# A Mamba-2 mixer and a LoRA dense layer on one core: one unit's transposes by VectorE in 32x32 blocks and through DRAM

## What is computed

```python
proj = einsum('bsd,ed->bse', layernorm(x), in_proj_w)       # gate | hs,B,C | dt
hBC  = silu(causal depthwise conv, 4 taps, of proj's middle part)
hs   = hBC[..., :8192].reshape(b, s, 128 heads, 64)         # B, C: 8 groups x 128
xch  = hs * softplus(dt)                                     # per token and head
Y_diag = (C B^T * L) @ xch          # in chunks of 128 tokens, L = decay, lower triangle
states = B^T @ (decay * xch)        # per chunk, then carried from chunk to chunk
Y_off  = C @ carried states * exp(A_cum)
Y = Y_diag + Y_off + hs * D
out = groupnorm(Y * silu(gate)) * norm_w @ out_proj_w.T
x = x + out; x = x + layernorm(x) @ (W + LoRA) + b
```

## Time and profile before

| what | value |
|---|---|
| median of 3 runs (lowest, highest) | 1605.16 us (1605.1, 1605.87) |
| span of the profiled execution | 1605.0 us |
| PE busy | 1583.5 us, 99% |
| DVE busy | 1264.2 us, 79% |
| ACT busy | 1163.1 us, 72% |
| POOL busy | 700.7 us, 44% |
| chain that ended last | PE 97%, DVE 1%, ACT 1% |
| mean granted TensorE clock | 0.998 of 2.4 GHz |
| DMA | 162.37 MB, mean 101 GB/s, q1 30.8% of the 16 engines |

### The profile page before, as it was taken

The page is one execution under the profiler, slowest core; times in us unless marked ns, Lnnn a source line. Parts: engine busy times, 40 slices in busy tenths (PEclk is TensorE's granted clock), DMA queues, the critical chain, the costliest instruction groups (busy, mean ns, idle before and its releaser), DMA issues.

```text
span 1605.0 us, 26714 instructions
## 1 busy us (share of the span) xinstructions
PE 1583.5 (99%) x9576; PEld 1346.1 (84%) x9576; DVE 1264.2 (79%) x1984; ACT 1163.1 (72%) x2027; POOL 700.7 (44%) x535
## 2 busy tenths in 40 slices
PE   7899999999999999999999999999999999999998
PEld 5688888888888888888888888888888888888887
DVE  6687777877778777887778877787877878788787
ACT  5887667776777677777687766777677767777753
POOL 2155444453444454354453544445344445435550
PEclk9999999999999999999999999999999999999999
DMA  4542322332323233332232232233232323223211
GB/s 151 192 145 86 122 89 83 112 112 73 112 97 114 73 109 95 98 106 92 99 108 97 86 122 89 83 112 112 73 112 99 113 73 109 99 92 112 93 44 53
DMA packets 86916, 162.37 MB, mean 101 GB/s; under 512 B 23040, under 2 KB 39424, under 8 KB 86528
## 3 DMA queue, kind: packets, MB, share of 16 engines
q1 hardware_dynamic: 86784, 160.66, 30.8%
HBM read 154.84 MB, written 5.77 MB: 100 GB/s over the span
## 4 chain that ended last, share of the span: by engine, by line
PE 97%; DVE 1%; ACT 1%; issue 0%; DMA 0%; SPq 0%; DVEq 0%; ACTq 0%
PE g_bank L778 10%; PE g_bank L780 9%; PE g_bank L779 9%; PE d_bank L797 7%; PE x_bank L778 7%; PE x_bank L780 7%; PE x_bank L779 7%; PE head_bank L786 5%; PE head_bank L804 5%; PE x_bank L836 4%; PE x_bank L837 4%; PE x_bank L835 4%; PE d_bank L837 4%; PE d_bank L835 4%; PE d_bank L836 4%; PE head_bank L812 3%
## 5 line engine op out<-in xcount | busy, mean ns | idle before, releaser
L1448 POOL TENSOR_TENSOR w_low<-raw,w_high 128x512 fp32r<-128x512 f32 x139 | 179.8, 1294 | 553.5 <-ACT w_high L1011 553.5
L1199 DVE SCALAR_TENSOR_TENSOR hs<-x_bank,cols,hs 128x1022 f32<-128x1022 f32 x189 | 241.6, 1278 | 129.7 <-ACT hs L1033 127.5
L1021 ACT ACTIVATE scores<-scores,tables 128x128 f32<-128x128 f32 x1024 | 312.4, 391 | 0.0
L1462 POOL TENSOR_TENSOR y<-y,gate 128x512 f32<-128x512 f32 x128 | 185.4, 1467 | 198.8 <-DVE y L1268 198.8
L1033 ACT ACTIVATE hs<-x_bank,cols 128x1024 f32<-128x1024 f32 x63 | 75.9, 1204 | 269.9 <-PE x_bank L780 269.9
L778 PE MATMUL g_bank<-x_high,w_high 128*128 128x512 f32 x624 | 250.8, 402 | 0.0
L779 PE MATMUL g_bank<-x_low,w_high 128*128 128x512 f32 x624 | 243.2, 390 | 0.0
L780 PE MATMUL g_bank<-x_high,w_low 128*128 128x512 f32 x624 | 243.1, 390 | 0.0
L778 PE MATMUL x_bank<-x_high,w_high 128*128 128x512 f32 x504 | 196.3, 390 | 0.1
L780 PE MATMUL x_bank<-x_high,w_low 128*128 128x512 f32 x504 | 196.1, 389 | 0.0
L779 PE MATMUL x_bank<-x_low,w_high 128*128 128x512 f32 x504 | 196.1, 389 | 0.0
(11 more groups left out here) (211 smaller groups left out, 3433.3 us busy)
## 6 DMA issues: line engine op xcount, KB each, us to landing
scores<-sums_dram SPq DMA_DIRECT2D x128, 512.0 KB, 4.8
raw<-w_in SPq DMA_DIRECT2D x144, 256.0 KB, 2.9
grown_rows<-grown_dram SPq DMA_DIRECT2D x256, 96.0 KB, 2.8
out_raw<-w_out SPq DMA_DIRECT2D x64, 256.0 KB, 3.4
mixed<-x SPq DMA_DIRECT2D x8, 256.0 KB, 5.1
out<-mixed SPq DMA_DIRECT2D x8, 256.0 KB, 2.0
table_dram<-table SPq DMA_DIRECT2D x2, 768.0 KB, 5.3
tables<-table_dram SPq DMA_DIRECT2D x30, 48.0 KB, 2.7
```

The source lines that it names most:

```text
L1021: op = s.activation(at, at, ACT.Relu, bias=col[:, r, c:c + 1], scale=-1.0)
L1199: v.scalar_tensor_tensor(out=hs[:, q % 2, :, i:], in0=x_bank[:, :, 0:SEQ - i], scalar=cols[:, q, TAPS - 1 - i:TAPS - i], in1=hs[:, q % 2, ...
L1448: pool.tensor_tensor(w_low[:, slot], raw[:, slot], w_high[:, slot].bitcast(F32), ALU.subtract)\
L1462: pool.tensor_tensor(y[:, b], y[:, b], gate[:, q % 2, b], ALU.mult).then_inc(y_ready, 1)
```

## The change

TensorE's `turn_hs` goes, except in the first unit (`turn_first`, `first_heads`). From the second unit on, VectorE transposes `hs` in 32x32 blocks in one instruction (`turn_blocks`), with the output ordered so that the four 32-token pieces m of every chunk lie together. It writes into the half of `hs` that the previous unit has left, after that unit's `skip`. SP stores this to DRAM (`store_blocks`, 128 rows of 4 KB). Four loads (`load_quads`, each 128 runs of 1 KB into 32 partitions) bring it back as `quads`, tokens on the partitions. `to_heads` now reads `quads` in SBUF, one product for each of the two heads over both batches. So `xdt` is ready for both batches at once.

The order moves with it. On VectorE the three taps are together, ahead of `carried_state`; `turn_blocks` follows `skip`; `to_heads` comes behind both scores, and `squares_of` behind `y_low_part`. On SP the store stands before the grown loads and the quad loads behind them; the first weight load of the unit after is moved ahead of the store. On ScalarE the silu of `hs` comes before the second `differences`, both `decays` come last, and tap 0 waits for the store two units back. TensorE waits for `carry_scaled` in `states`. The bias buffers share memory with `out_high` and `out_low` (not shown, with the changed argument lists).

```diff
@@ -34,6 +34,9 @@
 DMA_SCRATCH = 8192
+QUAD = 32
+QUADS = P // QUAD
+PER_HEAD = HEAD_DIM // QUAD
@@ -81,6 +84,13 @@
+def splits_after(g, last, j, by):
+    if j + by < UNITS:
+        return splits_of(g, last, j + by)
+    return [] if last else splits_of(g + 1, False, j + by - UNITS)
@@ -95,6 +105,7 @@
     dense_dram = scratch("dense_dram", [P, KT * HID])
+    blocks_dram = scratch("blocks_dram", [P, BATCH * SEQ])
@@ -618,13 +629,16 @@
         ident_r = sb("ident_r", [P, P], F32R)
-        bias_high, bias_low = sb("bias_high", [P, HID], F32R), sb("bias_low", [P, HID], F32R)
+        quads = sb("quads", [P, QUADS, BATCH, CHUNKS, QUAD])
+        bias_high, bias_low = out_high[:, 0], out_low[:, 0]
...
         chunk_in = [[sem(f"chunk_in{b}_{h}") for h in range(2)] for b in range(BATCH)]
+        blocks_turned, blocks_stored = sem("blocks_turned"), sem("blocks_stored")
+        moved = [sem(f"moved{m}") for m in range(QUADS)]
@@ -658,6 +672,10 @@
+        def blocks_of(k):
+            return hs[:, (k - 1) % 2].rearrange("p b n -> p (b n)")
@@ -688,6 +706,20 @@
+            def store_blocks(k):
+                sp.wait_ge(blocks_turned, k)
+                for m in range(QUADS):
+                    reached(sp, moved[m], 16 * (k - 1))
+                sp.dma_start(blocks_dram, blocks_of(k)).then_inc(blocks_stored, 16)
+            def load_quads(k):
+                sp.wait_ge(blocks_stored, 16 * k)
+                sp.wait_ge(xdt_ready, PAIR * k)
+                by_part = blocks_dram.rearrange("(a j) (m n) -> m j a n", a=QUADS, m=QUADS)
+                for m in range(QUADS):
+                    sp.dma_start(quads[m * QUAD:(m + 1) * QUAD].rearrange("p a b c i -> p a (b c i)"), by_part[m])\
+                      .then_inc(moved[m], 16)
@@ -714,14 +746,9 @@
                     ahead, second = unit(g, last, j + 1), unit(g, last, j + 2)
-                    if j + 1 < UNITS:
-                        splits = splits_of(g, last, j + 1)
-                    else:
-                        splits = [] if last else splits_of(g + 1, False, 0)
+                    splits = splits_after(g, last, j, 1)
...
                         first_dense(sp)
-                    for at in splits[:1]:
-                        load_weight(*at)
@@ -743,9 +770,16 @@
                         load_weight(*at)
+                    then = splits_after(g, last, j, 2)[:1]
+                    for at in then if len(splits) < SPLIT else []:
+                        load_weight(*at)
                     if ahead:
+                        store_blocks(ahead[2])
...
                             load_grown(ahead[2], b)
+                        load_quads(ahead[2])
+                    for at in then if len(splits) == SPLIT else []:
+                        load_weight(*at)
@@ -759,6 +793,8 @@
             load_weight(0, place(0, 2) + 1)
+            for at in splits_after(0, False, 0, 1)[:1]:
+                load_weight(*at)
@@ -782,6 +818,7 @@
                 pe.wait_ge(xdecay_ready, BATCH * k + b + 1)
+                reached(pe, carry_scaled, BATCH * (k - 1) + b + 1)
@@ -791,7 +828,7 @@
                 pe.wait_ge(scores_ready, BATCH * k + b + 1)
-                pe.wait_ge(xdt_ready, BATCH * k + b + 1)
+                pe.wait_ge(xdt_ready, PAIR * (k + 1))
@@ -805,11 +842,10 @@
-            def turn_hs(k, s, b):
-                pe.wait_ge(hs_ready, k + 1)
-                reached(pe, carry_scaled, BATCH * (k - 1) + b + 1)
+            def turn_first(b):
+                pe.wait_ge(hs_ready, 1)
                 for c in range(CHUNKS):
-                    mm = pe.transpose(head_bank[b][:, c * P:(c + 1) * P], hs[:, s, b, c * P:(c + 1) * P], ident[:])
+                    mm = pe.transpose(head_bank[b][:, c * P:(c + 1) * P], hs[:, 0, b, c * P:(c + 1) * P], ident[:])
@@ -893,8 +929,8 @@
                                 pe.wait_ge(bc_ready, 1)
-                                turn_hs(0, 0, 0)
-                                turn_hs(0, 0, 1)
+                                turn_first(0)
+                                turn_first(1)
@@ -937,9 +973,6 @@
                             project(g, (NEXT_B, NEXT_C)[j - 4], b, g_bank[:, b])
-                    if ahead:
-                        for b in range(BATCH):
-                            turn_hs(k + 1, (j + 1) % 2, b)
@@ -1030,6 +1063,7 @@
                 reached(s, skip_added, k - 1)
+                reached(s, blocks_stored, 16 * (k - 1))
@@ -1140,8 +1174,8 @@
                         differences(k + 1, ahead[0], ahead[1], 0)
-                        decays(k + 1, ahead[1], 0)
                         silu_hs(k + 1, (j + 1) % 2)
+                        differences(k + 1, ahead[0], ahead[1], 1)
@@ -1150,14 +1184,15 @@
                     if ahead:
-                        differences(k + 1, ahead[0], ahead[1], 1)
-                        decays(k + 1, ahead[1], 1)
+                        for b in range(BATCH):
+                            decays(k + 1, ahead[1], b)
...
                         s.wait_ge(bias_in, 16)
-                        s.activation(bias_high[:], bias_row, ACT.Copy).then_inc(bias_high_ready, 1)
+                        s.wait_ge(out_done, CHUNKS * (ALL - 2))
+                        s.activation(bias_high, bias_row, ACT.Copy).then_inc(bias_high_ready, 1)
@@ -1268,16 +1303,36 @@
-            def to_heads(g, q, k, b):
-                if q % HALF == 0:
-                    v.wait_ge(tables_in[b][q // HALF], 16 * (g + 1))
-                v.wait_ge(turned, BATCH * k + b + 1)
-                reached(v, diag_done, BATCH * (k - 1) + b + 1)
-                reached(v, xdecay_ready, BATCH * (k - 1) + b + 1)
-                col = table_of(DT, b, q).rearrange("p r c -> p c r")
+            def first_heads(b):
+                v.wait_ge(tables_in[b][0], 16)
+                v.wait_ge(turned, b + 1)
+                col = table_of(DT, b, 0).rearrange("p r c -> p c r")
...
+            def turn_blocks(k):
+                v.wait_ge(hs_ready, k + 1)
+                v.wait_ge(skip_added, k)
+                v.transpose(blocks_of(k).rearrange("p (m n i) -> p n m i", m=QUADS, i=QUAD),
+                            hs[:, k % 2].rearrange("p b (c m i) -> p (b c) m i", c=CHUNKS, i=QUAD))\
+                 .then_inc(blocks_turned, 1)
+            def to_heads(g, q, k):
+                for m in range(QUADS):
+                    v.wait_ge(moved[m], 16 * k)
+                v.wait_ge(diag_done, BATCH * k)
+                v.wait_ge(xdecay_ready, BATCH * k)
+                if q % HALF == 0:
+                    for b in range(BATCH):
+                        v.wait_ge(tables_in[b][q // HALF], 16 * (g + 1))
+                for r in range(PAIR):
+                    col = tables[:, :, q // HALF, DT, PAIR * (q % HALF) + r]
+                    v.tensor_tensor(xdt[:, :, :, r],
+                                    quads[:, r * PER_HEAD:(r + 1) * PER_HEAD].rearrange("p h b c i -> p (b c) h i"),
+                                    col.unsqueeze(3).to_broadcast([P, BATCH, CHUNKS, HEAD_DIM]), ALU.mult)\
+                     .then_inc(xdt_ready, 1)
@@ -1359,10 +1414,9 @@
-                    for b in range(BATCH):
-                        to_heads(g, j, k, b)
-                    if j == 1 and g > 0:
-                        squares_of(g)
+                    if k == 0:
+                        for b in range(BATCH):
+                            first_heads(b)
@@ -1375,23 +1429,26 @@
                         score(g, j, k, 1)
+                    if k > 0:
+                        to_heads(g, j, k)
...
                     if j == 1 and g > 0:
+                        squares_of(g)
...
                     if ahead:
-                        tap(1, *ahead)
+                        for i in range(1, TAPS):
+                            tap(i, *ahead)
...
                     if ahead:
-                        tap(2, *ahead)
-                        tap(3, *ahead)
                         skip(j, k)
+                        turn_blocks(k + 1)
@@ -1463,7 +1520,7 @@
                 u = BATCH * k + b
-                pool.wait_ge(xdt_ready, u + 1)
+                pool.wait_ge(xdt_ready, PAIR * (k + 1))
```

10 lines of the change are left out of this document (5 added, 5 removed).

## The result

The changed kernel takes **1688.53 us** (median of 4 runs, 1687.36 to 1691.77) against 1605.13 (1605.02 to 1605.87): 1.0521 times, 95% interval 1.0506 to 1.0536. It is slower by 83 us where 27 us faster was forecast, and 86 us above the upper end of the range (1603).

A forecast was written before the change was run, and what follows sets the result against it. TensorE, busy 99% of the span, was taken as the bound. 1605.0 - 54.8 (transposes) + 19.6 (second to fourth units) + 8.4 (sixth and seventh) = 1578.2 us of span, 1578.4 as median; range 1554 to 1603.

The forecast's parts named there:

- What is removed, 54.8 us: TensorE: eight transposes a unit, 0.87 us, leave the chain in 63 units, 54.8 us in all.
- The operations added: VectorE's transpose at 1.2 us, store landing at 4.0, quad issues at 0.6 and landing at 3.1.
- Typical unit: stall 0, with hardly a margin: Unit of 21.17 us: first decay done at X+21.1 (X: projection's end), TensorE asks at X+21.17, so no stall.
- first decay 0.85 us later: GpSimd: the first decay ends 0.85 us after xdt is done at X+20.2, so at X+21.1.
- Both ways lead to X+14.05 for the first quad load: SP's queue: store landed by X+14.05, grown loads issued by X+14.0; the first quad load follows.
- Second to fourth units, 2.8 a group: VectorE's squares and normed blocks delay tap 1; stalls of 1.0, 0.9, 0.9 us in seven groups, 19.6 us.
- Sixth and seventh units, 0.6 each: VectorE: xdt behind the B or C taps stalls TensorE 0.6 us in each of fourteen units, 8.4 us.
- two microseconds late, less the one by which TensorE was held: Third unit's tap 1 comes two microseconds late; less TensorE's own delay, 0.9 us more at the fourth unit's states.
- The new stalls cost clock: Rival, 2%: a half-clock stretch of 4 us costs 2; in all 35 held units +70, 1648 us.
- 63 units less 0.87: TensorE: every unit but the first loses its 0.87 us of transposes, 54.8 us in all.
- Rival (c): Slower, 11%: the round trip becomes the bound; 0.95 us longer eats the gain, 2 us longer gives 1651.
- At nothing: Counted as free: late exponentials, weight and output loads, waits for the store and carry_scaled, bias buffers, added bytes.

The follow-up runs named there:

- e5: e1 with xdt (to_heads) put back ahead of the B or C taps in the sixth and seventh units of a group; 1603.61 us, ratio 0.9992.
- e1: The changed kernel with SP issuing the four quad loads right behind the store, ahead of the grown loads; 1626.55 us, ratio 1.0136.
- e8: e6 with SP's queue order as in the change, grown loads ahead of the quad loads; 1663.86 us, ratio 1.0361.
- e4: The changed kernel with quads read from another DRAM tensor, ahead of the store and not waiting for it (output wrong); 1609.46 us, ratio 1.0029.
- e6: e5 with the six normed blocks of third and fourth units moved behind the block transpose; 1594.74 us, ratio 0.9934.
- e7: e6 with y_low moved from behind to_heads to behind the three taps; 1593.92 us, ratio 0.9921.
- e9: e6 with xdt ahead of the second batch's score on VectorE; 1613.04 us, ratio 1.0047.
- e10: e7 with xdt ahead of the second batch's score on VectorE; 1608.93 us, ratio 1.0025.

## Why the prediction was wrong, point by point

- **What is removed, 54.8 us: right.** 504 matmuls are gone, and where nothing stalls the interval is shorter by just this (27.5 to 26.6 in e5).
- **The operations added: right.** Transpose 1.245 us for 1.2. Store landing 2.6 for 4.0, quads 3.0 for 3.1, issues 0.43 to 0.49 for 0.6. The DMA terms all erred on the safe side. The Trainium skill, DMA: Bandwidth & Descriptors, section Anatomy of one DMA, gave 3.2 and 2.3 as an estimate (for issue from GpSimd, while SP issues here): the trace puts the store below it and the loads above. Read as eight transposes, the figure of the Trainium skill, VectorE: DVE Perf Modes, section The three transpose paths, gave an estimate of 2.5 us where the row has 1.245.
- **"Typical unit: stall 0, with hardly a margin": the first step that failed.** The walk was a ring that returned to the states at X+21.1, and it was closed with 0.07 us to spare. Taken from states to states, its pieces were off as follows: carry 9.15 after the states for 8.90; first quad load 14.53 for 14.05; xdt 4.73 behind it for 4.9; and xdt to states **3.25 for 2.15**. The last is the term that was mis-sized: "first decay 0.85 us later". It came from the decays of before, which ran beside nothing of that kind; put beside y_low, the first takes 1.81. Sum of the misses 1.4 us: 22.5 for 21.1. The trace of before had a warning: in the second and third unit of the first group its decays do run beside the scores and y_low, and four of the 128 take 1.8 us. GpSimd, then VectorE, in the second unit:

```profile
85.45 3.61 POOL L1469 TENSOR_TENSOR xdecay<-xdt,tables 128x384 f32<-128x384 f32 x2
...
85.19 3.16 DVE L1231 TENSOR_TENSOR scores<-scores,bc 128x1024 f32<-128x1024 f32 x2
88.28 1.86 DVE L1215 SCALAR_TENSOR_TENSOR y_low<-y,cols,y_high 128x1024 fp32r<-128x1024 f32 x1
```

- **"Both ways lead to X+14.05 for the first quad load": the second step that failed, and the dearest.** The time itself was nearly right (14.53, of which 0.25 is carry's). But the store's landing was taken too long by 1.4 us, and this hid that the grown loads, which wait for the same unit's sums, were alone what held the quads. The text even said that a stall pushes carry, sums, grown loads and quads; it didn't draw from it that a ring through the queue turns every delay of TensorE into one of the next unit. e1 and e8 put 62 and 69 us on the queue's order.
- **Second to fourth units, 2.8 a group: too small.** Measured, intervals 2-3 to 4-5 are 2.4, 3.5 and 3.4 above before less 0.87, not 1.0, 0.9 and 0.9. The normed blocks were taken at 0.7 each from the earlier trace rows; three took 4.25 us beside GpSimd. What was called "two microseconds late, less the one by which TensorE was held" isn't forgiven: VectorE's row is itself part of the ring.
- **Sixth and seventh units, 0.6 each: right in kind, wrong in size.** 28.5 less 26.6 is 1.9 a unit, 27 us and not 8.4. The place was right (e5 gets 23 back), the difference is again the first decay beside y_low (1.81 for 0.85) and xdt at 1.3 for 1.2.
- **"The new stalls cost clock", 2%: it did happen, in part.** The price was nearly right, 1.7 us for a low stretch where 2 was said, but in 11 places and at the end, not in all 35: 23.7 us more missing clock in all. The case against it rested on stalls of 0.5 to 1 us; those that brought a fall were 1.97 and more. By the Trainium skill, Perfetto Trace Analysis, section Matmul Optimizations, matmuls should run back to back; the trace agrees in kind, 0.72 of the clock for the 6 us behind a 2.05 us gap, though the 2.78 us gap shown above brought no fall.
- **First and last group: not in the sum.** Two short units at the start and one at the end took 18.6, 18.6 and 16.6 us before and 23.8, 24.3 and 21.2 after. The formula "63 units less 0.87" supposed TensorE to be the bound in all; in a unit with less to compute the late xdt and the trip lie bare. Order and trip have about equal parts: e4, without the wait on the trip, has 20.7, 19.8 and 20.5, 7 us more than before, and the change 8 us more than e4. e6 has 22.9, 22.4 and 20.5, 12 us more than before.
- **Rival (c), 11%**, had the right shape and side (the round trip as the bound) but put it on late landings, which were early. "At nothing" held otherwise, as far as the waits tell: VectorE's scores waited 1.4 us in all for the exponentials, and no wait for the bias or the weight loads shows among those quoted.

How the 55 us went: e6 keeps 11. From e6 to the changed kernel the queue's order is 69, the other two misplacements (e5, e6) 32 from e1 on, and these overlap in part, the whole being 94. What e6 still lacks (44) is by the table 11 in the first group, 8 in the last and some 23 in the six between; of the last, which part is the decay beside y_low and which VectorE's row was not told apart, as e7, e9 and e10 each moved the wait elsewhere.

## What to carry to other kernels

When work leaves the bound engine for a round trip, write the trip as a ring from that engine back to itself, with every queue position in it, and compare its length with the engine's own period; a walk that ends "just in time" has no forecast in it. In a queue that waits in order, a transfer goes behind nothing that waits for later work than it does itself: here one line's place was worth 62 to 69 us. And take no duration from a row where the operation ran alone if the new order puts it beside the other elementwise engine; look first for its slowest cases in the same trace, which here held four decays of 1.8 us among 128.
